# The edges' totals: TensorE makes them one mixing step later, VectorE reads them behind a block of statistics

## The chip, the cores and the metric

One core of one Trainium2 chip runs the whole program. The metric is the device time of one execution in microseconds (us). The kernel before takes 763.93 us (median of three executions, 762.85 to 764.43).

## The reference

The inputs are x (6250 rows of 256 numbers), a graph of 100,000 edges given as `src`, `dst` and `edge_weight`, and weights. Three parts are added up.

```
xn = layernorm(x)
m  = product of 100,000 plane rotations, edge by edge; edges outside the first 256 rows or columns fall away
x1 = x + xn @ m.T + mix(xn)        # mix: K = xn Wk + bk, softmax over the 6250 rows, lambda = softmax(K).T @ (xn Wv + bv),
                                   #      normalised, then (xn Wq + bq) @ lambda
x2 = x1 + moe(layernorm(x1))       # 8 experts, the top 2 of each row, 256 -> 512 -> 256
```

Only edges with an end below 256 change the rotation matrix. So the kernel first sorts out which of the 100,000 edges count, numbers them, and gathers their records; that is the "edge work" of the first part. The change lies there.

## The kernel before

Each engine has its own list of instructions, written out by hand, and the lists meet at semaphores. Nothing reorders them: an instruction that waits holds back all that stands behind it on its engine.

**The mixing steps.** The rows of x are taken in 13 groups, group 0 of 106 rows and groups 1 to 12 of 512. For a group q:

- VectorE makes the mean and variance of the rows (`row_stats`, line 1302 for the statistics, line 1305 to combine them; `xld2` and `xld3` are the third and fourth blocks of eight row tiles of x).
- ScalarE turns the variance into a scale (`deviations`), and normalises the rows (`norm_rows`, line 981).
- TensorE transposes the normalised rows (`turn_in`, line 2199), and multiplies them with the key weights (`keys`, line 2208).
- VectorE takes the running maximum of the keys (`maxima`, lines 1337 to 1347; line 1346 writes `ebias`, for which ScalarE waits), ScalarE takes the exponentials (`exps`, line 1029), TensorE transposes them (`turn_exps`, line 2219), ScalarE moves them to SBUF (`turned_exps`, line 1019), and TensorE multiplies them with the rows (`weigh`, line 2229).
- VectorE adds that product to a running sum (`weighted_sum`, line 1360), which frees the PSUM bank.

TensorE's `mix_step(q)` is `turn_exps(q)`, `keys(q+1)`, `turn_in(q+2)`, then a piece of edge work in some steps, then `weigh(q)`. `weigh(q)` waits until `weighted_sum(q-1)` of VectorE has emptied the bank. VectorE's `mix_step(q)` is `weighted_sum(q-1)`, `sum_exps(q)` (lines 1351 to 1354), `maxima(q+1)`. Edge work stands between the mixing steps on VectorE as well.

**The edge work around the change.** VectorE counts, in each of up to 125 partitions, the edges that matter (`count_rest`, `count_head`, the last instruction being the scan of line 1399). TensorE makes the totals over the partitions with eight small matmuls against a triangle and against ones (`totals`, line 2237), into the first four columns of the bank `misc`. VectorE copies the four columns to SBUF and compares two of them with bounds (`take_counts`: line 1404, then lines 1406 and 1407). GpSimd waits for that copy (`TOTALLED`). It adds the totals to the numbers of the edges (lines 747 and 748), reports `ENDS`, and goes on with passes over all 100,000 edges (lines 750, 751, 726, 727, 726, 727, 731, 757). VectorE's `split_ends` (lines 1412 to 1416) waits for `ENDS`; `hist_columns(0)` (line 1420, 125 x 3200) follows it, and `mix_step(2)` follows that.

In the order of TensorE before, `totals` stands in step 1:

```
for q = 1:  turn_exps(1)  keys(2)  turn_in(3)  totals()  weigh(1)
for q = 2:  turn_exps(2)  keys(3)  turn_in(4)  weigh(2)
```

Later, in step 5, TensorE makes `pair_totals` (line 2261) by six matmuls of one column each, which are like those of `totals`. ScalarE takes sines and cosines of all edges ahead of `end_step(4)`; GpSimd gathers records once VectorE's `number_blocks` is done in step 4.

Of the kernel before, what the change touches and what calls it, by code (L numbers as in the profile page):

```python
# [21 lines left out]
def gnn_layer(nc, x, src, dst, edge_weight, W_qk, b_qk, W_v, b_v, bn_gamma, bn_beta,  # L22
              gamma, beta, Wr, br, W1, b1, W2, b2, out):

    N, D = x.shape
    NE = src.shape[0]
    NX, _, H = W1.shape
    KB = D // P
    NT = (N + P - 1) // P
# [52 lines left out]
    with ctx:  # L82
# [300 lines left out]
        S = {}  # L383
# [905 lines left out]
        def _(dve):  # L1289
# [8 lines left out]
            def row_stats(loaded, lo, hi):  # L1298

                dve.wait_ge(S[loaded], 16)  # L1300
                for t in range(lo, hi):
                    last = nc.vector.bn_stats(stats[:, t, :], x_all[:, t, :])  # L1302
                own(last)
                for t in range(lo, hi):
                    last = nc.vector.bn_aggr(mv[:, t, :], stats[:, t, :])
                return last
# [25 lines left out]
            def maxima(q):  # L1332
                W = width(q)
                n0 = q * PERM + base
                dve.wait_ge(S["keys_psum"], q + 1)
                for kb in range(KB):
                    last = nc.vector.reduce_max(grp_m[:, kb:kb + 1], bank[2 + kb][:, 0:W], AX_X)
                last.then_inc(S["dve"], 1)
                dve.wait_ge(S["dve"], n0 + 1)
                at_least(dve, S["exp_done"], q)  # L1340
                STT(new_m[:, :], run_m[:, :], 1.0, grp_m[:, :], ALU.mult, ALU.max).then_inc(S["dve"], 1)
                dve.wait_ge(S["dve"], n0 + 2)
                STT(dm[:, :], run_m[:, :], 1.0, new_m[:, :], ALU.mult, ALU.subtract)
                STT(ebias[:, :], bk_c[:, :], 1.0, new_m[:, :], ALU.mult, ALU.subtract).then_inc(S["dve"], 1)
                dve.wait_ge(S["dve"], n0 + 3)
                STT(ebias[:, :], ebias[:, :], 1.0, bk_c[:, :], ALU.mult, ALU.subtract).then_inc(S["ebias_ready"], 1)
                STT(run_m[:, :], new_m[:, :], 1.0, new_m[:, :], ALU.mult, ALU.max)

            def sum_exps(q):
                dve.wait_ge(S["exp_done"], q + 1)  # L1350
                STT(ssum[:, :], ssum[:, :], 1.0, alpha[:, :], ALU.mult, ALU.mult).then_inc(S["dve"], 1)
                dve.wait_ge(S["dve"], q * PERM + (base + 4))
                STT(ssum[:, :], ssum[:, :], 1.0, gsum[:, :], ALU.mult, ALU.add)
                STT(alpha2[:, :], alpha[:, :], 1.0, alpha[:, :], ALU.mult, ALU.max).then_inc(S["dve"], 1)
                dve.wait_ge(S["dve"], q * PERM + (base + 5))

            def weighted_sum(q):
                dve.wait_ge(S["mix_psum"], q + 1)
                for kb in range(KB):
                    last = STT(Pacc[:, kb, :], Pacc[:, kb, :], alpha2[:, kb:kb + 1], bank[6][:, kb * D:(kb + 1) * D],  # L1360
                               ALU.mult, ALU.add)
                last.then_inc(S["mix_acc"], 1)
            def mix_step(q):

                if q > 0:
                    weighted_sum(q - 1)
                if q == 4:
                    number_blocks()
                sum_exps(q)
                if q + 1 <= NG12:  # L1370
                    maxima(q + 1)
# [29 lines left out]
            def take_counts():  # L1401

                dve.wait_ge(S["pe"], 1)
                nc.vector.tensor_copy(sums4[:, :], misc[:, 0:4]).then_inc(S["edge_dve"], 1)
                dve.wait_ge(S["edge_dve"], TOTALLED)
                TS(bad[:, 1:2], sums4[:, 2:3], RC * P + 0.5, None, ALU.is_gt)
                TS(bad[:, 2:3], sums4[:, 3:4], HC * P + 0.5, None, ALU.is_gt)

            def split_ends():

                dve.wait_ge(S["edge_pool"], ENDS)
                el(TS(ends_hi[:, :], ends_f[:, :], -(P - 0.5) / 2, 1.0 / P, ALU.add, ALU.mult))
                el(TS(ends_hi[:, :], ends_hi[:, :], MAGIC, None, ALU.add))
                el(TS(ends_hi[:, :], ends_hi[:, :], -MAGIC, None, ALU.add))
                nc.vector.tensor_copy(ends_hi16[:, :], ends_hi[:, :])
                STT(ends_lo[:, :], ends_hi[:, :], -float(P), ends_f[:, :], ALU.mult, ALU.add).then_inc(S["edge_dve"], 1)
                dve.wait_ge(S["edge_dve"], SPLIT)
# [15 lines left out]
            def number_blocks():  # L1433

                dve.wait_ge(S["edge_pe"], BASES)
                el(nc.vector.tensor_copy(counted[:, :], misc[:, 3 * P:3 * P + NCH]))
                for c0, c1 in ((0, HC), (HC, NCH)):
                    last = nc.vector.tensor_tensor_scan(upsum[:, c0:c1], ones[:, 0:1].broadcast_to([P, c1 - c0]), counted[:, c0:c1], 0.0, ALU.mult, ALU.add)
                el(last)
                el(TT(upsum[:, :], upsum[:, :], counted[:, :], ALU.subtract))  # L1440
                TT(block_of[:, :], upsum[:, :], misc[:, 2 * P:2 * P + NCH], ALU.add).then_inc(S["edge_dve"], 1)
# [156 lines left out]
            count_head()  # L1598
            row_stats("xld2", 16, 24)
            mix_step(1)  # L1600
            take_counts()
            row_stats("xld3", 24, 32).then_inc(S["xstats_ok"], 1)
            split_ends()
            hist_columns(0)
            mix_step(2)
# [581 lines left out]
        def _(pe):  # L2187
# [4 lines left out]
            def turn_in(q, b):  # L2192

                W = width(q)
                nt, r = (W + P - 1) // P, W % P or P
                pe.wait_ge(S["xn_ready"], q + 1)
                for kb in range(KB):
                    for t in range(nt):
                        last = tr(bank[kb][:, t * P:t * P + r], xng[b][0:r, t, kb * P:(kb + 1) * P], ident[0:r, 0:r])
                last.then_inc(S["xT_psum"], 1)  # L2200

            def keys(q):
                W = width(q)
                pe.wait_ge(S["xT_done"], q + 1)
                at_least(pe, S["exp_done"], q)
                for db in range(KB):
                    for kb in range(KB):
                        last = mm(bank[2 + db][:, 0:W], wk[:, kb, db * P:(db + 1) * P],  # L2208
                                  xnT[:, kb, bass.ds(tile_at(q) * P, W)], start=(kb == 0), stop=(kb == KB - 1))
                last.then_inc(S["keys_psum"], 1)  # L2210

            def turn_exps(q):

                W = width(q)
                nt, r = (W + P - 1) // P, W % P or P
                pe.wait_ge(S["exp_done"], q + 1)
                for kb in range(KB):
                    for t in range(nt):
                        last = tr(bank[4 + kb][0:r, t * P:(t + 1) * P], ex[:, kb, t * P:t * P + r], ident[:, :])  # L2219
                last.then_inc(S["exT_psum"], 1)  # L2220
# [12 lines left out]
            def totals():  # L2233

                pe.wait_ge(S["edge_dve"], HEAD_SUMMED)
                for c, (left, right, n) in enumerate(((tri, incl, EP), (tri, h_incl, HP), (ones, incl, EP), (ones, h_incl, HP))):
                    last = mm(misc[:, c:c + 1], left[0:n, :], right[:, right.shape[1] - 1:right.shape[1]], start=True, stop=True)
                last.then_inc(S["pe"], 1)

            def histogram():  # L2240

                pe.wait_ge(S["edge_dve"], HIGH)
                for c in range(PH):
                    mm(misc[:, P:P + HC], head_lo[:, c, :], head_hi[:, c, :], start=(c == 0), stop=(c == PH - 1))
                for c in range(PB):
                    last = mm(misc[:, P + HC:P + NCH], hist_lo[c // half_c][:, c % half_c, :], hist_hi[c // half_c][:, c % half_c, :],
                              start=(c == 0), stop=(c == PB - 1))
                last.then_inc(S["edge_pe"], 1)
# [38 lines left out]
            def mix_step(q, b):  # L2287
                turn_exps(q)
                if q + 1 <= NG12:
                    keys(q + 1)  # L2290
                if q + 2 <= NG12:
                    turn_in(q + 2, (b + 2) % 3)
                if q == 1:
                    totals()
                if q == 3:
                    histogram()
                if q == 5:
                    pair_totals()
                weigh(q, b)
# [357 lines left out]
```

## Time and profile before

| what | before |
|---|---|
| median of three executions | 763.93 us |
| the profiled execution | 764.22 us |
| its span, from the first to the last instruction | 762.4 us |
| TensorE busy | 649.5 us (85%) |
| VectorE busy | 508.6 us (67%) |
| ScalarE busy | 443.9 us (58%) |
| GpSimd busy | 407.6 us (53%) |
| mean granted clock of TensorE | 0.921 |

The shares are means over a long kernel. The change touches only some 10 us of it, between 37 and 62 us of the span, so the order of time there says more than the shares do. The chain of waits follows the work that ended last back from the last instruction. The timeline lists one engine's instructions in order of time, and says in brackets how long the engine sat idle ahead of one and what ended that idle time.

### The profile page before, as it was taken

What the parts mean: (1) busy time and instruction counts of PE and PEld (TensorE: products, weight loads), DVE (VectorE), ACT (ScalarE), POOL (GpSimd) and SP (SyncE); (2) the same over time, 40 slices, a digit from 0 to 9 for tenths busy, and PEclk for the clock granted to TensorE, in tenths of its full rate; (3) what the DMA queues carried; (4) which work ended last, traced back from release to release, by engine and by line L of the source; (5) the groups of instructions that cost most, each with busy time, mean ns of one, the idle gap of its engine ahead of it and who ended that gap; (6) DMA issues with size and microseconds to landing.
All of it is one profiled execution on the core that took longest, in us unless ns stands there. A gap on an engine that the chain in (4) does not pass through costs nothing.

```text
span 762.4 us, 18086 instructions
## 1 busy us (share of the span) xinstructions
PE 649.5 (85%) x4055; PEld 552.4 (72%) x4056; DVE 508.6 (67%) x1934; ACT 443.9 (58%) x1218; POOL 407.6 (53%) x494
## 2 busy tenths in 40 slices
PE   6679799944369898807999999999979999999997
PEld 5356467632257666506998999899969999999996
DVE  4999758869957688853454444444446777777775
ACT  6446676557313177844666666566645666666663
POOL 7763777235411237770666677523335666666655
PEclk7879899975579999957999999999999999999999
DMA  6802011415620045562344333322213333333322
GB/s 197 257 2 85 19 33 27 122 52 190 202 71 1 29 144 183 192 209 65 120 141 135 115 131 118 103 69 69 67 63 101 99 104 102 98 103 101 110 91 65
DMA packets 60749, 79.72 MB, mean 105 GB/s; under 512 B 15719, under 2 KB 49381, under 8 KB 60319
## 3 DMA queue, kind: packets, MB, share of 16 engines
q1 hardware_dynamic: 45145, 43.27, 19.6%
q0 software_dynamic: 14976, 35.38, 13.9%
q10 hardware_dynamic: 576, 0.54, 0.2%
q14 instruction: 40, 0.33, 0.1%
q8 instruction: 12, 0.20, 0.1%
HBM read 47.53 MB, written 33.13 MB: 106 GB/s over the span
## 4 chain that ended last, share of the span: by engine, by line
PE 60%; DVE 21%; issue 7%; DMA 4%; ACT 3%; POOL 2%; SPq 1%; DVEq 1%; POOLq 0%; ACTq 0%
PE banks L2601 22%; PE banks L2611 20%; PE banks L2229 4%; PE banks L2208 3%; PE banks L2592 3%; PE banks L2553 2%; DVE R L1997 2%; DVE R L1742 1%; DVE R L1420 1%; DMA R<-in_x_dram 1%; DVE topi L2023 1%; DVE R L1757 1%; DVE R L1302 1%; DMA R<-send_d 1%; PE banks L2219 1%
## 5 line engine op out<-in xcount | busy, mean ns | idle before, releaser
L2601 PE MATMUL banks<-R 128*128 128x128 f32 x1696 | 210.1, 278 | 2.8 <-ACT R L1251 2.8
L2601 PEld LDWEIGHTS banks<-R 128*128 128x128 f32 x1696 | 200.7, 194 | 3.7 <-ACT R L1251 3.6
L2611 PE MATMUL banks<-R 128*128 x848 | 200.7, 380 | 0.0
L1264 ACT ACTIVATE R<-banks,b1c 128x128 f32<-128x128 f32 x424 | 143.5, 365 | 52.0 <-PE banks L2601 51.8
L2611 PEld LDWEIGHTS banks<-R 128*128 128x128 f32 x848 | 153.4, 191 | 16.5
L1251 ACT ACTIVATE R<-banks,bet_c,gam_c 128x128 f32<-128x128 f32 x212 | 85.7, 454 | 106.1 <-PE banks L2592 103.3
L2116 DVE COPY R<-R 128x1024 f32 x106 | 74.5, 702 | 77.2 <-PE banks L2601 60.9
L899 POOL DMA_INDIRECT send_d<-R,slot_all x98 | 97.1, 991 | 48.1 <-issue 40.8
L912 POOL DMA_INDIRECT first_d<-R,dest_now x54 | 60.7, 1123 | 93.3 <-DVE R L2121 81.7
L921 POOL DMA_INDIRECT R<-first_d,get_now x52 | 53.8, 1034 | 50.6 <-DVE get_now L2098 46.3
L912 POOL DMA_INDIRECT out_dram<-R,dest_now x52 | 64.4, 1239 | 30.4 <-issue 27.1
L2229 PE MATMUL banks<-R 128*128 128x256 f32 (+1 forms) x196 | 51.7, 423 | 14.8 <-ACT R L1019 7.4
L2229 PEld LDWEIGHTS banks<-R 128*128 128x128 f32 (+1 forms) x196 | 40.9, 214 | 22.7 <-ACT R L1019 10.3
L2121 DVE TENSOR_TENSOR R<-banks,R 128x256 f32<-128x256 f32 x54 | 22.9, 425 | 49.9 <-PE banks L2611 49.9
L2592 PE MATMUL banks<-ident,R 128*128 128x128 f32 x212 | 41.3, 277 | 15.5 <-DMA R<-send_d 15.5
L2553 PE MATMUL banks<-comb,R 128*128 128x274 f32 (+1 forms) x196 | 51.7, 393 | 0.0
L2592 PEld LDWEIGHTS banks<-ident,R 128*128 128x128 f32 x212 | 29.7, 142 | 27.6 <-DMA R<-send_d 12.2
L2208 PE MATMUL banks<-R 128*128 128x512 f32 (+1 forms) x104 | 46.8, 594 | 0.6 <-ACT R L1009 0.6
L1263 ACT ACTIVATE R<-R 128x256 f32 x106 | 43.3, 408 | 2.7 <-DVE R L2141 2.7
L2110 DVE TENSOR_SCALAR R<-R 128x256 f32<-128x256 f32 x106 | 43.2, 408 | 0.0
L2553 PEld LDWEIGHTS banks<-comb,R 128*128 128x128 f32 (+1 forms) x196 | 33.6, 189 | 9.0
L801 POOL DMA_INDIRECT R<-erec_d,R x33 | 33.8, 1024 | 11.0 <-issue 9.4
(545 smaller groups left out, 998.4 us busy)
## 6 DMA issues: line engine op xcount, KB each, us to landing
R<-send_d SPq DMA_DIRECT2D x106, 131.0 KB
R<-in_L_ffn_W_dram SPq DMA_DIRECT2D x16, 512.0 KB, 4.5
R<-in_x_dram SPq DMA_DIRECT2D x14, 512.0 KB, 4.3
R<-in_x_dram SPq DMA_DIRECT2D x5, 1024.0 KB, 10.8
send_d<-zrow SPq DMA_DIRECT2D x14, 131.0 KB, 2.4
send_d<-R,slot_all POOLq DMA_INDIRECT x98, 3.1
erec_d<-R SPq DMA_DIRECT2D x1, 1400.0 KB
rec_d<-R SPq DMA_DIRECT2D x1, 1400.0 KB
```

The lines of the kernel that those rows point to most:

```text
L899: nc.gpsimd.indirect_dma_start(out=send_d, out_offset=bass.IndirectOffsetOnAxis(ap=slot_all[0:r, t, c:c + 1], axis=0), in_=row_all[0:r, t, ...
L912: nc.gpsimd.indirect_dma_start(out=into, out_offset=bass.IndirectOffsetOnAxis(ap=dest_now[b][:, :], axis=0), in_=yb[b], in_offset=None, bo ...
L921: nc.gpsimd.indirect_dma_start(out=firsts[b], out_offset=None, in_=first_d, in_offset=bass.IndirectOffsetOnAxis(ap=get_now[b][:, :], axis= ...
L1251: last = nc.scalar.activation(xmT[b][:, kb * P:(kb + 1) * P], bank[b][:, kb * P:(kb + 1) * P], ACT.Identity, bias=bet_c[:, kb:kb + 1], sca ...
L1264: last = nc.scalar.activation(hT[b][:, c, :], bank[2 + 2 * b + c // 2][:, (c % 2) * P:(c % 2 + 1) * P], ACT.Gelu, bias=b1c[:, bass.ds(e, 1 ...
L2116: nc.vector.tensor_copy(w1c[b].rearrange("p k h -> p (k h)"), w1s[:, bass.ds(e, 1), :, :].rearrange("p a k h -> p (a k h)"))\
L2208: last = mm(bank[2 + db][:, 0:W], wk[:, kb, db * P:(db + 1) * P], xnT[:, kb, bass.ds(tile_at(q) * P, W)], start=(kb == 0), stop=(kb == KB ...
L2229: last = mm(bank[6][:, kb * D:(kb + 1) * D], exT[0:r, t, kb * P:(kb + 1) * P], xng[b][0:r, t, :], start=(t == 0), stop=(t == nt - 1))
L2553: last = mm(into, xnT[:, kb, at:at + r], comb[:, kb, :], start=False, stop=(kb == KB - 1))
L2592: last = tr(bank[b][:, kb * P:(kb + 1) * P], xm[b][:, kb * P:(kb + 1) * P], ident[:, :])
L2601: last = mm(bank[2 + 2 * b + c // 2][:, (c % 2) * P:(c % 2 + 1) * P], w1c[b][:, kb, c * P:(c + 1) * P], xmT[b][:, kb * P:(kb + 1) * P], st ...
L2611: last = mm(bank[6 + b][:, 0:D], hT[b][:, c, :], w2s[:, bass.ds(e, 1), c, :].rearrange("p a h -> p (a h)"), start=(c == 0), stop=(c == H / ...
```

## The change

`totals()` on TensorE moves from mixing step 1 to step 2. On VectorE `take_counts()` moves behind the statistics of the fourth block of x. No instruction is added or removed; the eight matmuls, the copy and the two comparisons, their waits and their signals are the same.

```
@@ VectorE's list
             row_stats("xld2", 16, 24)
             mix_step(1)
+            row_stats("xld3", 24, 32).then_inc(S["xstats_ok"], 1)
             take_counts()
-            row_stats("xld3", 24, 32).then_inc(S["xstats_ok"], 1)
             split_ends()
             hist_columns(0)
             mix_step(2)
@@ TensorE's mix_step(q, b)
                 if q + 2 <= NG12:
                     turn_in(q + 2, (b + 2) % 3)
-                if q == 1:
+                if q == 2:
                     totals()
                 if q == 3:
                     histogram()
```

## Rows read from the trace of the kernel before

**Rows 1.** Chain of waits, 50 to 84 us: start, duration, engine, tile, line.

```profile
50.35 4.08 DVE R L1420
54.43 0.78 DVE R L1360 x2
70.04 1.34 ACT R L1029 x4
82.37 1.08 ACT R L1019 x2
83.49 6.72 PE banks L2229 x16
```

**Rows 2.** Timeline of TensorE: start, duration, engine, line, operation, out<-in, count, idle before.

```profile
30.83 1.04 PE L2199 MATMUL banks<-ident,R 128*128 128x128 f32 x8
37.30 1.01 PE L2237 MATMUL banks<-R,tri 125*128 125x1 f32 x4 [5.42 <-DVE R L1399]
38.17 0.99 PE L2237 MATMUL banks<-R,ones 125*128 125x1 f32 x4
41.42 5.57 PE L2229 MATMUL banks<-R 128*128 128x256 f32 x16 [2.26 <-DVE R L1360]
...
51.14 1.04 PE L2199 MATMUL banks<-ident,R 128*128 128x128 f32 x8
55.35 5.38 PE L2229 MATMUL banks<-R 128*128 128x256 f32 x16 [3.18 <-DVE R L1360]
```

**Rows 3.** Timeline of TensorE, `pair_totals` and what follows it.

```profile
95.24 0.28 PE L2261 MATMUL banks<-R,tri 125*128 125x1 f32 x2
...
95.83 3.70 PE L2229 MATMUL banks<-R 128*128 128x256 f32 x16
```

**Rows 4.** Timeline of VectorE, 40 to 61 us.

```profile
40.43 0.84 DVE L1360 SCALAR_TENSOR_TENSOR R<-R,alpha,banks 128x256 f32<-128x256 f32 x2
...
43.58 0.15 DVE L1404 COPY sums<-banks 128x4 f32<-128x4 f32 x1
...
43.90 2.70 DVE L1302 BATCH_NORM_STATS2 R<-R 128x6 f32<-128x256 f32 x8
...
47.20 0.16 DVE L1412 TENSOR_SCALAR R<-R 125x55 f32<-125x55 f32 x1
...
48.44 1.75 DVE L1415 CAST R<-R 125x55 bf16<-125x55 f32 x1
...
50.35 4.08 DVE L1420 TENSOR_TENSOR R<-R 125x3200 bf16<-125x3200 bf16 x1
54.35 0.86 DVE L1360 SCALAR_TENSOR_TENSOR R<-R,alpha,banks 128x256 f32<-128x256 f32 x2
55.13 1.04 DVE L1351 SCALAR_TENSOR_TENSOR ssum<-ssum,alpha 128x2 f32<-128x2 f32 x1
...
56.28 1.42 DVE L1354 SCALAR_TENSOR_TENSOR alpha<-alpha 128x2 f32<-128x2 f32 x1
...
59.06 0.63 DVE L1341 SCALAR_TENSOR_TENSOR new_m<-run_m,grp_m 128x2 f32<-128x2 f32 x1
...
59.99 0.16 DVE L1346 SCALAR_TENSOR_TENSOR ebias<-ebias,bk_c 128x2 f32<-128x2 f32 x1
```

**Rows 5.** Timeline of GpSimd, from the totals to its last pass.

```profile
44.37 0.27 POOL L748 TENSOR_SCALAR R<-R,sums 70x5 f32<-70x5 f32 x1
44.84 1.73 POOL L750 TENSOR_SCALAR R<-R,sums 125x800 f32<-125x800 f32 x1 [0.20 <-POOL R L748]
...
58.05 1.63 POOL L757 TENSOR_TENSOR R<-R 125x800 f32<-125x800 f32 x1 [0.18 <-POOL R L731]
```

**Rows 6.** Windows: stretch; busy PE, PEld, DVE, ACT, POOL; PEclk; DMA share; GB/s.

```profile
45.00:46.00 1.00, 1.00 (x6) 0.90 (x5) 1.00 (x4) 0.17 (x2) 1.00 (x1) 0.88 0.00 0
...
54.35:69.90 15.55, 13.50 (x102) 10.13 (x103) 15.17 (x34) 5.62 (x14) 5.05 (x3) 0.89 0.32 104
...
83.40:87.00 3.60, 3.51 (x8) 2.86 (x9) 3.53 (x3) 2.45 (x8) 3.10 (x2) 0.50 0.08 18
```

More of the change, by code:

```diff
@@ L1600, in _ @@
             mix_step(1)
+            row_stats("xld3", 24, 32).then_inc(S["xstats_ok"], 1)
             take_counts()
-            row_stats("xld3", 24, 32).then_inc(S["xstats_ok"], 1)
             split_ends()
@@ L2292, in mix_step @@
                     turn_in(q + 2, (b + 2) % 3)
-                if q == 1:
+                if q == 2:
                     totals()
```

## The prediction

> **What bounds the kernel now.** I read the chain of waits first, because a change of order can only matter where the end of the kernel is set. From 50 us on it runs through VectorE: `hist_columns(0)` at 50.35, the weighted sum at 54.43, then by ScalarE's exponentials at 70.04 to the moved exponentials at 82.37 and TensorE's `weigh(4)` at 83.49 [rows 1]. So in the stretch of the change VectorE sets the end, not TensorE. The windows say the same: of the 15.55 us from 54.35 on VectorE is busy for 15.17 [rows 6]. It has no idle time there in which a delay could vanish.
>
> The timeline of TensorE shows the reverse. It is done with `turn_in(3)` at 31.9, sits 5.42 us until the totals can start, ends them at 39.2, and then sits another 2.26 us until VectorE's weighted sum; `weigh(1)` starts at 41.42. After `turn_in(4)`, which ends at 52.2, it is idle again for 3.18 us, for VectorE's next weighted sum [rows 2]. TensorE is ahead of VectorE, waiting.
>
> The timeline of VectorE gives the order that the change edits: the copy of the totals at 43.58, some 4.4 us after TensorE finished them, with no wait; the statistics of the fourth block from 43.90; `split_ends` from 47.20 [rows 4].
>
> **The change on TensorE, step 1.** Taking the totals out of step 1 removes a wait of 5.42 us and 1.9 us of matmuls. What is late next is the weighted sum: `weigh(1)` must have the bank that VectorE empties in line 1360, and that runs at 40.43 for 0.84 us [rows 4], behind the statistics of the third block. So `weigh(1)` still starts at 41.4, and the removed wait is worth nothing. Its cover is VectorE's order, which the change leaves as it is up to that point.
>
> One side effect can cost. The engine now idles from 31.9 to 41.4 at a stretch. In the trace `weigh(1)` takes 5.57 us and `weigh(2)`, after an idle stretch of 3.18 us, takes 5.38 [rows 2]; `weigh(4)` starts with a granted clock of 0.50 for its first 3.6 us, the 1.2 GHz level, and takes 6.72 us [rows 1, 6]; in `weigh(1)` the clock has risen to a mean of 0.88 by 45 to 46 us [rows 6]. So `weigh(1)` will take between 5.38 and 6.72 us, a cost of -0.2 to +1.15 us. I take +0.5, the mean of the two ends (6.05) less 5.57.
>
> **The change on TensorE, step 2.** Behind `weigh(1)` TensorE has `turn_exps(2)`, `keys(3)` and `turn_in(4)`, all of which have their inputs (`turn_in(4)` ran without a wait), and then the totals. The next matmul after `turn_in(4)` could start at 52.0: rows that follow one another overlap by some 0.15 us, so that is 52.18 less that. Six matmuls of `pair_totals`, of the same kind, take from 95.24 to 95.83 at the high clock, 0.10 us each [rows 3]; eight take 0.8 us. The result is there at 52.9 to 53.0, and VectorE's copy can start at 53.05. With the slower `weigh(1)` that is 53.55. The totals stay ahead of `weigh(2)`, whose input from VectorE comes far later, so their 0.8 us delays nothing on TensorE itself.
>
> **The change on VectorE.** `mix_step(1)` ends at 43.6 as before. The statistics of the fourth block then run 0.3 us earlier and end at 46.9 (3.3 us, from 43.90 to 47.20 [rows 4]). Their signal wakes ScalarE's `deviations(4)`, which by its own order stands behind the end of `weigh(1)`, so earlier is worth nothing. Then the copy of the totals waits for TensorE, from 46.9 to 53.05: 6.1 us of idle time on the engine that sets the end. Queued behind it on VectorE are the two comparisons, `split_ends`, `hist_columns(0)` and the whole of `mix_step(2)`. For the last of these TensorE's `weigh(2)` and ScalarE's `exps(3)` wait. GpSimd waits for the same copy, so its edge passes start as much later as the copy does.
>
> There is a second new wait. `split_ends` needs `ENDS` of GpSimd, which comes when line 748 ends: 44.64, or 1.06 us after the copy starts [rows 4, 5]. Before, the statistics covered it. Now it lies open. `split_ends` and `hist_columns(0)` together took from 47.20 to 54.35, 7.15 us. So the weighted sum starts at 53.05 + 1.06 + 7.15 = 61.26 instead of 54.35, which is **6.9 us later**.
>
> **GpSimd's passes beside VectorE.** Some of VectorE's small instructions were stretched while GpSimd had a pass over the edges. Of `mix_step(2)`, line 1351 took 1.04 us, line 1354 1.42 and line 1341 0.63, where line 1346, on the same 128x2, took 0.16 [rows 4]: 0.9 + 1.25 + 0.45 = 2.6 us lost. The last pass ended at 59.68 [rows 5]. Relative to `ENDS` the passes last 15.0 us, and VectorE spent the first 2.56 of these (44.64 to 47.20) in the statistics, which were not stretched. That cover goes. The bounds are -2.6 us, if no pass meets `mix_step(2)`, and +2.6 us, if all that the statistics covered falls on stretched instructions. Laid side by side with the durations of the trace, `split_ends` and `hist_columns(0)` meet lines 750, 751 and 726 and come out as long as before; `mix_step(2)` then meets lines 727, 726, 727 and 731 in place of 727, 731 and 757, and `ebias` comes 6.8 to 8.0 us after the weighted sum starts, in place of 5.8. I take **+1.2 us**, near the lower end of these 1.0 to 2.2.
>
> The rule behind such stretches in the Trainium skill (SBUF — State Buffer, section on who interferes with whom) is that VectorE and GpSimd share a pair of ports as an exclusive lock: an instruction with two SBUF inputs, or in a two-port mode, is blocked for the whole of a GpSimd instruction that came first, and the statistics, with one input, are not. The cast of line 1415, 1.75 us on 125x55, agrees with it [rows 4]. By the rule the extra is what the alignment gives; without it the extra would be 0, and the forecast 1.2 us lower.
>
> **What comes later.** From the weighted sum on, all chains hang on VectorE: maxima, exponentials, the later edge work, the start of GpSimd's gathers, and by way of ScalarE's sines `weigh(4)`. ScalarE's waits for GpSimd's passes (at 71.4 before) keep their margin: the last pass will end near 69.2, and ScalarE comes there near 80. I find nothing with a start of its own in time that could take the delay up: x is loaded by then, and the gathers start from VectorE's numbers. So the delay is carried whole to the end.
>
> The sum: 0.5 (clock) + 6.9 (the wait, and `ENDS` uncovered) + 1.2 (GpSimd's passes) = +8.6 us. Against the profiled execution of 764.22 that is 772.8. Its span of 762.4 leaves 1.8 us outside, which I leave as it is. The profiled execution is 0.3 us above the median, so for the median I say 772.5.
>
> **The rivals.**
>
> *Part of the delay is taken up later (7 in 100).* TensorE sits idle ahead of `weigh(4)`, and further on in the mixing steps VectorE waits for TensorE. If one of these stretches were tied to something that doesn't move, up to some 5 us would come back. Against it: ahead of `weigh(4)` the chain runs over ScalarE, whose work starts from `exps(4)` and thus from VectorE [rows 1]. The time would be 764.2 + 3.5, so 767.5 or so, in 765.5 to 769.5.
>
> *TensorE gets ahead by the wait that is removed (5 in 100): no slower, or faster.* If `weigh(1)` could start when `turn_in(3)` ends, at 31.9, the totals would stand 10.6 us later (52.0 less 41.42), at 42.5 plus 0.8. They would be ready before the statistics end at 46.9, and VectorE would wait for nothing. Only the uncovered `ENDS` (1.06 us) would stay, and against it up to 2.6 us of stretched instructions could go: 761.5 to 765. It decides from the point at which `weigh(1)` starts by 35.4, for 35.4 + 10.6 + 0.9 is 46.9. For it speaks that TensorE idled longest at the totals. Against it, the row of `weigh(1)` names VectorE's line 1360 as what ended the last wait [rows 2], and that line stands behind the third block's statistics. The start would have to be 6 us earlier than that.
>
> *It costs more (5 in 100).* A `weigh(1)` and a `weigh(2)` at the low clock throughout, and 2.6 us from GpSimd's passes: 0.5 + 1.15 + 6.9 + 2.6 = 11.2, or 775.4, and up to 777.
>
> **How the numbers follow.** The forecast has 83 in 100, with a range of its own of 769.5 to 775 (6.9 alone less some tenths, to 6.9 + 1.15 + 2.6). The range for 8 in 10 is the same, 769.5 to 775, since the rivals hold 17 in 100 among them. A measurement of this kernel tells about 0.2% (1.5 us) from no change. Slower by more: 0.93, from the forecast, the dearer case and nearly all of the first rival with part of the chance of the time in between. Within it: 0.04. Faster by more: 0.03.
>
> **What would show each step.** In the timeline after: `weigh(1)` still starts at 41.4 and ends at 47 to 48; no idle wait for line 1399 at TensorE; totals at 52 to 53.5; VectorE idle some 6 us ahead of line 1404, released by TensorE's line 2237, and 0.8 us ahead of line 1412, released by GpSimd; the weighted sum of `mix_step(2)` at 61 to 62; `weigh(4)` at 92 where it was at 83.49. The prediction is wrong if `weigh(1)` starts clearly before 41, if VectorE waits for the totals by under 3 us, or if `weigh(4)` moves by much less than the weighted sum does.

## The result, and the profile after

The changed kernel takes 769.64 us (median of 19, 763.89 to 773.52), the kernel before, on the same chips, 762.73 us (median of 19, 757.41 to 765.84). The ratio is 1.0106, with a 95% interval of 1.0085 to 1.0128: 8.1 us slower, 6.5 to 9.8. (8.1 us is the centre of this interval; the two medians lie 6.9 us apart.) The forecast was +8.6. Some executions fall in a slower state of the chip; all ratios below, and the time of e10, go by the others alone.

The two profiled executions differ by 2.1 us only (764.22 and 766.33). One reason is that the after one got through the loads earlier: its weighted sum of mixing step 1 starts at 35.91 where it started at 40.43 before [rows 4]. VectorE's statistics of the second block waited for x for 3.54 us before and for 0.56 after, and in the other profiles this weighted sum starts anywhere from 34.92 to 41.66. So I compare stretches counted from this weighted sum, not times from the start.

The chain of waits of the changed kernel, 35 to 89 us (start, duration, engine, tile, line; short stretches of "issue" are left out):

```profile
35.99 0.77 DVE R L1360 x2
36.90 6.58 PE banks L2229 x16
43.48 0.87 PE banks L2219 x8
44.35 3.44 PE banks L2208 x8
47.79 0.87 PE banks L2199 x8
48.66 0.80 PE banks L2237 x8
49.48 0.17 DVE sums L1404
49.83 0.35 POOL R L747
50.28 0.28 POOL R L748
...
53.09 3.49 DVE R L1420
...
60.70 1.49 DVE new_m L1341
...
64.17 1.52 DVE nmr L1319
...
88.58 6.35 PE banks L2229 x16
```

This is the change in one view. Before, the chain ran through VectorE here. Now it crosses to TensorE at `weigh(1)`, goes through all of TensorE's queue ahead of the totals (lines 2229, 2219, 2208, 2199), over the totals and their copy, and on over GpSimd's two small additions to `split_ends` of VectorE, on which it stays until ScalarE's exponentials.

The timeline of TensorE, where `weigh(1)`, the totals, `weigh(2)` and `weigh(4)` answer to [rows 2] and [rows 1]:

```profile
36.90 6.58 PE L2229 MATMUL banks<-R 128*128 128x256 f32 x16 [7.51 <-DVE R L1360]
...
48.50 0.50 PE L2237 MATMUL banks<-R,tri 125*128 125x1 f32 x4
48.86 0.58 PE L2237 MATMUL banks<-R,ones 125*128 125x1 f32 x4
57.51 6.51 PE L2229 MATMUL banks<-R 128*128 128x256 f32 x16 [8.07 <-DVE R L1360]
```

The wait of 5.42 us for line 1399 is gone, and nothing came of it: the idle time ahead of `weigh(1)` is one stretch of 7.51 us, ended as before by VectorE's line 1360. The timeline of VectorE, against [rows 4]:

```profile
41.79 0.64 DVE L1305 BATCH_NORM_AGGREGATE mv<-R 128x2 f32<-128x6 f32 x8
49.48 0.16 DVE L1404 COPY sums<-banks 128x4 f32<-128x4 f32 x1 [7.05 <-PE banks L2237]
...
50.63 0.19 DVE L1412 TENSOR_SCALAR R<-R 125x55 f32<-125x55 f32 x1 [0.73 <-POOLq L749]
...
52.73 0.29 DVE L1415 CAST R<-R 125x55 bf16<-125x55 f32 x1
...
53.09 3.49 DVE L1420 TENSOR_TENSOR R<-R 125x3200 bf16<-125x3200 bf16 x1
56.50 0.87 DVE L1360 SCALAR_TENSOR_TENSOR R<-R,alpha,banks 128x256 f32<-128x256 f32 x2
...
57.47 1.80 DVE L1353 SCALAR_TENSOR_TENSOR ssum<-ssum,gsum 128x2 f32<-128x2 f32 x1
...
62.29 1.42 DVE L1344 SCALAR_TENSOR_TENSOR ebias<-bk_c,new_m 128x2 f32<-128x2 f32 x1
...
64.17 1.52 DVE L1319 SCALAR_TENSOR_TENSOR nmr<-mv,rstd 128x16 f32<-128x16 f32 x1
```

Two waits that were not there, 7.05 us for the totals and 0.73 us for `ENDS`. The instructions around them lie differently against GpSimd's passes: the cast and `hist_columns(0)` are short now, four small instructions of 128x2 and 128x16 long. The timeline of GpSimd, for comparison:

```profile
53.17 4.13 POOL L726 TENSOR_SCALAR R<-R 125x800 f32<-125x800 f32 x1 [0.20 <-POOL R L751]
57.38 1.87 POOL L727 TENSOR_TENSOR R<-R 125x800 f32<-125x800 f32 x1
...
60.29 1.87 POOL L727 TENSOR_TENSOR R<-R 125x800 f32<-125x800 f32 x1
62.25 1.62 POOL L731 TENSOR_SCALAR R<-R 125x800 f32<-125x800 f32 x1
64.05 1.61 POOL L757 TENSOR_TENSOR R<-R 125x800 f32<-125x800 f32 x1 [0.18 <-POOL R L731]
```

Line 1353 of VectorE starts 0.09 us behind the pass at 57.38 and ends with it (57.47 + 1.80 = 59.27, the pass 59.25). Lines 1341 (60.70 to 62.18) and 1319 (64.17 to 65.69) end in the same way with the passes at 60.29 and 64.05 (62.16 and 65.66), and line 1344 ends 0.16 us ahead of the one at 62.25. The weighted sum of step 3, in the changed kernel:

```profile
71.72 0.86 DVE L1360 SCALAR_TENSOR_TENSOR R<-R,alpha,banks 128x256 f32<-128x256 f32 x2
```

and in the kernel before:

```profile
66.62 0.86 DVE L1360 SCALAR_TENSOR_TENSOR R<-R,alpha,banks 128x256 f32<-128x256 f32 x2
```

From the weighted sum of step 1 to that of step 3 it is 35.81 us (71.72 less 35.91), in place of 26.19 (66.62 less 40.43 [rows 4]).

### The profile page after: what moved, and what is told of

The parts are those of the page before. It is cut to its first block, busy times and chain, and to the rows that moved or that the text cites. A ratio compares the mean times of both kernels' runs of the same rounds, so it can differ in the third digit from the quotient of the medians.

```text
span 764.5 us, 18086 instructions
## 1 busy us (share of the span) xinstructions
PE 646.1 (85%) x4055; PEld 549.2 (72%) x4056; DVE 507.8 (66%) x1934; ACT 442.9 (58%) x1218; POOL 406.7 (53%) x494
## 4 chain that ended last, share of the span: by engine, by line
PE 61%; DVE 20%; issue 8%; DMA 4%; ACT 3%; POOL 2%; SPq 1%; DVEq 1%; POOLq 0%; ACTq 0%
PE banks L2601 21%; PE banks L2611 20%; PE banks L2229 5%; PE banks L2208 4%; PE banks L2592 3%; PE banks L2553 2%; DVE R L1997 2%; DVE R L1742 1%; DMA out_dram<-R,dest_now 1%; DVE topi L2023 1%; PE banks L2219 1%; DVE R L1420 1%; DVE R L1757 1%; DMA R<-send_d 1%; DMA R<-in_x_dram 1%
## 5 line engine op out<-in xcount | busy, mean ns | idle before, releaser
L2229 PE MATMUL banks<-R 128*128 128x256 f32 (+1 forms) x196 | 53.4, 433 | 24.4 <-DVE R L1360 17.5
L2592 PEld LDWEIGHTS banks<-ident,R 128*128 128x128 f32 x212 | 29.6, 143 | 27.5 <-DMA R<-send_d 12.6
```

The lines of the kernel that those rows point to most:

```text
L2229: last = mm(bank[6][:, kb * D:(kb + 1) * D], exT[0:r, t, kb * P:(kb + 1) * P], xng[b][0:r, t, :], start=(t == 0), stop=(t == nt - 1))
L2592: last = tr(bank[b][:, kb * P:(kb + 1) * P], xm[b][:, kb * P:(kb + 1) * P], ident[:, :])
```

## The experiments

Times are medians; the ratio is to the kernel before on the same chip. It is the centre of its interval and not the quotient of the two medians: for e11 the medians lie 3.5 us apart and the ratio says 1.0. "Way" is the stretch from the weighted sum of step 1 to that of step 3 in the profile: 26.19 us before, 35.81 changed. The first four ran on a chip where the kernel before took 763.0 us, the next four on one where it took 822.6, the last four on one with 763.65. The 823 us chip is slower later in the program for all kernels, and only ratios and ways are taken from it.

| run | time | ratio (95%) | in us | way | wait ahead of line 1404 |
|---|---|---|---|---|---|
| e1, TensorE's half | 771.15 | 1.0111 (1.0065 to 1.0156) | +8.5 | 36.32 | 10.14 |
| e2, VectorE's half | 765.47 | 1.0035 (1.0003 to 1.0067) | +2.7 | 28.68 | none |
| e3, totals first | 765.76 | 1.0042 (1.0012 to 1.0072) | +3.2 | 30.79 | 2.02 |
| e4, ten more matmuls | 771.89 | 1.0128 (1.0087 to 1.0168) | +9.8 | 37.99 | 9.24 |
| e5, no idle | 830.56 | 1.0093 (1.0056 to 1.0130) | +7.7 | 34.63 | 5.84 |
| e6, warm `weigh(4)` | 821.0 | 0.9992 (0.9967 to 1.0017) | -0.7 | 26.15 | none |
| e7, changed, fewer passes | 826.94 | 1.0051 (1.0020 to 1.0082) | +4.2 | 30.75 | 6.91 |
| e8, before, fewer passes | 818.61 | 0.9952 (0.9918 to 0.9985) | -3.9 | 23.56 | none |
| e9, before, early passes | 764.64 | 1.0009 (0.9978 to 1.0040) | +0.7 | 23.56 | none |
| e10, changed, early passes | 767.2 | 1.0083 (1.0035 to 1.0131) | +6.3 | 30.97 | 4.48 |
| e11, early and warm | 760.15 | 0.9987 (0.9954 to 1.0019) | -1.0 | 26.27 | none |
| e12, e6 again | 761.73 | 0.9974 (0.9951 to 0.9998) | -2.0 | 26.15 | none |

**e1: TensorE's half alone.**

```
-                if q == 1:
+                if q == 2:
                     totals()
```

> TensorE's half of the change alone: totals in mixing step 2, take_counts of VectorE in its old place. Theory W (VectorE's wait for the totals is the cost): the copy of the totals waits from 43.6 to about 53, 9.4 us instead of 6 to 7, and the statistics behind it cover ENDS again, so +9 to +10 us on the kernel before. Rival P (the cost is VectorE's own reordering: ENDS uncovered, GpSimd's passes beside mix_step(2)): without that reordering less than the whole change, +3 us or less. Rival C (the cost is TensorE's clock after the long idle stretch): about the same as the whole change, +7 to +8.

VectorE waits longer than in the whole change, 10.14 us, as the statistics no longer stand ahead of the wait. No wait for `ENDS` is left, and `hist_columns(0)` and line 1351 are as long as before to 0.01 us:

```profile
50.13 0.16 DVE L1404 COPY sums<-banks 128x4 f32<-128x4 f32 x1 [10.14 <-PE banks L2237]
...
53.75 0.16 DVE L1412 TENSOR_SCALAR R<-R 125x55 f32<-125x55 f32 x1
...
56.83 4.08 DVE L1420 TENSOR_TENSOR R<-R 125x3200 bf16<-125x3200 bf16 x1
```

The way grows by 10.13 us, which is the wait of 10.14. Theory P is out. The time alone (+8.5, 5.0 to 11.9) would not have told W from C; the wait does.

**e2: VectorE's half alone.** The same edit the other way round: `take_counts()` moved, `totals()` in step 1.

> VectorE's half alone: take_counts behind the statistics of the fourth block, totals of TensorE in step 1 as before. Theory W: no wait for the totals; only ENDS lies open (+0.8 net) and GpSimd's passes meet mix_step(2) (+1.2), so +2.0 us, 0.8 to 3.5, on the kernel before. Rival P: +5 us or more. Rival C: 0.

```profile
46.39 0.12 DVE L1404 COPY sums<-banks 128x4 f32<-128x4 f32 x1
...
47.50 0.19 DVE L1412 TENSOR_SCALAR R<-R 125x55 f32<-125x55 f32 x1 [0.74 <-POOLq L749]
```

The way grows by 2.5 us, the time by 2.7 (0.2 to 5.1). So of the 9.6 us of the whole change 2.5 come from VectorE's order and 7.1 from the wait of 7.05. The two halves run alone add up to more, 12.6 us, since in e1 the statistics no longer hide 3.1 us of the wait. The 2.5 us are 0.45 us less up to step 2, although 0.74 us of waiting for `ENDS` is in there, and 2.9 us more from step 2 to step 3.

**e3: the totals first in step 2.**

```
             def mix_step(q, b):
+                if q == 2:
+                    totals()
                 turn_exps(q)
...
-                if q == 2:
-                    totals()
                 if q == 3:
```

> The whole change, but totals at the head of TensorE's mixing step 2, ahead of turn_exps(2), keys(3) and turn_in(4), which take 5.2 us. Theory W: the wait ahead of line 1404 falls by 4.5 to 5 us, to about 2.3, and the time is 4.7 us below the changed kernel, +3.4 us on the kernel before. Rival P and rival C: as the changed kernel, +7 to +8, since VectorE's order and TensorE's idle stretch ahead of weigh(1) are the same.

```profile
41.54 6.73 PE L2229 MATMUL banks<-R 128*128 128x256 f32 x16 [7.29 <-DVE R L1360]
48.10 0.50 PE L2237 MATMUL banks<-R,tri 125*128 125x1 f32 x4
```

TensorE's idle stretch and its slow `weigh(1)` are those of the changed kernel, but the wait is 2.02 us and the way 30.79: 5.03 us of wait less, 5.02 us of way less. This also bounds theory C: with the same clock most of the cost is gone.

**e4: the other way.** Ten idle matmuls of `ident` ahead of the totals.

> The whole change with ten idle 128x128 matmuls of ident ahead of the totals, whose product nobody reads (20 records of 0.115 us at the high clock, 2.3 us). Theory W: VectorE's wait grows by 2.3 us and the kernel by the same, +10.4 us on the kernel before. Rival (part of the delay is taken up later): less than 1.2 us above the changed kernel. Rival C: no more than the changed kernel, as TensorE's idle stretch ahead of weigh(2) only gets shorter.

The wait is 9.24 us, 2.19 more than in the changed kernel, and the way 2.18 longer. Four wait lengths (0, 2.02, 7.05, 9.24) with VectorE's new order give ways of 28.68, 30.79, 35.81 and 37.99: the way is 28.7 plus the wait, to 0.1 us. In the time the step from the changed kernel is +1.7 us, 2.3 were expected; the interval of e4 (6.6 to 12.8) is too wide to confirm it or to exclude the rival.

**e5: TensorE kept busy.** In step 1 28 idle matmuls after `turn_in(3)`, in step 2 26 more after the copy of the totals.

> The whole change with idle matmuls of ident that fill TensorE's two idle stretches: 28 in step 1 after turn_in(3), 26 in step 2 once VectorE has copied the totals. Their product is read by nobody. Theory C (part of the cost is the low clock after idle time): weigh(1) takes 3.7 us in place of 6.58, the totals come 2.9 us earlier, VectorE's wait falls from 7.05 to about 4.2, and the kernel gains 2.9 us on the changed one (+5.2 us on the kernel before). Rival: the clock there costs nothing, because some other wait holds the totals; then the time is that of the changed kernel, +8.

```profile
31.70 6.42 PE L2295 MATMUL banks<-ident 128*128 128x128 f32 x56
40.93 5.38 PE L2229 MATMUL banks<-R 128*128 128x256 f32 x16 [2.81 <-DVE R L1360]
```

The experiment half missed: the filling ended 2.81 us before `weigh(1)` could start, and the granted clock, 1.00 until 41 us, fell again (the windows show 0.60 from 41 to 43 us). `weigh(1)` took 5.38 us in place of 6.58, the wait 5.84 in place of 7.05, and the way 34.63 in place of 35.81: again one for one. So what `weigh(1)` takes less at the higher clock, 1.2 us here, is gained through the wait. The time (+7.7, 4.6 to 10.7) can't show that; it agrees with the theory and with the rival.

**e7 and e8: four of GpSimd's passes left out.** The angles miss the second and third parts of the whole turns.

```
             whole_turns(turn, theta)
             less_part(turn, theta, part_turn, TURN_HI)
...
-            less_part(turn, theta, part_turn, TURN_MID)
-            less_part(turn, theta, part_turn, TURN_LO)
```

> The changed kernel without four of GpSimd's passes over all edges: the second and third parts of the whole turns are not taken off the angles (lines 726 and 727, twice), so the angles are slightly off. Theory: GpSimd's passes stretch VectorE's small instructions of mix_step(2); without four of them mix_step(2) gets shorter by 2.5 to 3.5 us here. Against the same kernel with the old order (the next one) it is +6.5 to +7.5 us, which is the pure wait. Rival: the passes cost nothing, the time is that of the changed kernel (+8 on the kernel before) and the difference to the next one is 8.

> The kernel before without the same four passes of GpSimd. In its trace the stretched instructions of mix_step(2) lose 2.6 us and hist_columns(0) some 0.6 more; theory: -2 to -3 us on the kernel before. Rival: the stretched instructions are not on the path, 0.

In the old order the way falls by 2.63 us, in the new one by 5.06. Without the passes the change costs 7.19 us of way, with them 9.62: their share in it is 2.4 us. That the passes cost time shows in the times as well, -3.9 us for e8 (-6.7 to -1.2). The difference between e7 and e8 in the times is 8 us, with an interval too wide to tell 7.2 from 9.6.

**e9 and e10: the same passes, early.** The four passes go ahead of GpSimd's wait for the totals, where it sat idle for 8.5 us. Nothing is left out.

```
+            less_part(turn, theta, part_turn, TURN_MID)
+            less_part(turn, theta, part_turn, TURN_LO)
             pool.wait_ge(S["edge_dve"], TOTALLED)
```

> The kernel before with four of GpSimd's passes (lines 726 and 727, twice) moved ahead of its wait for the totals, into 8.5 us in which it sat idle; nothing is left out. Theory (the passes cost by stretching VectorE's instructions of mix_step(2), which sets the end): the way from the weighted sum of step 1 to that of step 3 falls from 26.2 to 23.6 us, and the kernel gains 2.5 to 3.7 us on the kernel before. Rival: the passes now stretch mix_step(1) as much, 0.

> The changed kernel with the same four passes moved ahead of GpSimd's wait for the totals. Theory: the change costs 7.2 us by VectorE's waits and 2.4 us more by the passes; with the passes out of the way the way between the two weighted sums falls from 35.8 to 30.8 us and the kernel is 3 to 4.5 us slower than before. Rival (the passes cost nothing extra in the changed order): +5 us or more.

The way is what was expected for both (23.56 and 30.97). The time of e9 is not: +0.7 (-1.7 to +3.1), where a gain of 2.5 to 3.7 us was expected. That of e10, +6.3 (2.7 to 10.0), holds the theory's 3 to 4.5 and the rival's 5 alike. In the profile of e9 the passes stand beside `count_head`, ahead of the way:

```profile
33.62 1.86 DVE L1397 SCALAR_TENSOR_TENSOR R<-R 70x79 f32<-70x79 f32 x1
35.52 0.90 DVE L1398 SCALAR_TENSOR_TENSOR R<-R 70x80 f32<-70x80 f32 x1
36.45 2.01 DVE L1399 TENSOR_TENSOR_SCAN R<-ones,R 70x80 f32<-70x80 f32 x1
```

These three took 0.23, 0.24 and 0.32 us in the kernel before: 4 us more here. Other instructions of `count_head` were long in the kernel before, line 1391 with 1.93 us for one, so the two profiles don't balance to the tenth; that the gain was given back there is the likely reading, not a shown one. Behind that point this profile keeps the gain: from the weighted sum of step 1 to the last instruction it is 3.0 us shorter than the kernel before.

Where the loads come early the passes fall beside `mix_step(1)` instead. That is so in the profile of e10, where a line 1351 took 1.69 us; its `mix_step(1)` is 2.6 us longer, and the wait for the totals, down to 4.48 from 7.05, hides nearly all of it. It is so in the profile of e11 below as well, which has VectorE's old order and no such wait: its way is 26.27 us, against 23.56 in e9 and 26.19 before. There the whole gain is gone, as e9's rival had it.

**e6, e12 and e11: a `weigh(4)` at the high clock.** This came out of [rows 1] and [rows 6]: `weigh(4)` is on the chain and took 6.72 us.

```
+                if q == 4:
+                    pe.wait_ge(S["edge_dve"], BLOCKS)
+                    for _ in range(22):
+                        mm(misc[:, 3 * P:4 * P], ident[:, :], ident[:, :], start=True, stop=True)
                 weigh(q, b)
```

> The kernel before with 22 idle matmuls of ident in TensorE's step 4, after number_blocks and ahead of weigh(4), in the 5.6 us for which TensorE waits for ScalarE; nobody reads their product. If the low clock of weigh(4) (6.72 us, on the chain) is a cost of its own, weigh(4) takes 3.7 us and the kernel becomes 2.5 to 3 us faster than before. Rival: weigh(4)'s length is covered by VectorE's edge work, which ends at 89.4 where weigh(4) ends at 90.2: then under 1 us.

> The kernel before with the four early passes and the 22 idle matmuls ahead of weigh(4). If both gains are there and add up: 4.5 to 6 us faster than the kernel before. Rival: weigh(4)'s gain is taken up by a later wait, then as the early passes alone, -2.5 to -3.7.

> The kernel before with the 22 idle matmuls ahead of weigh(4) once more, beside the others. In the first trace of it weigh(4) took 3.72 us in place of 6.72 and weigh(5) started 2.3 us earlier, but the time did not show it. Theory: -2.3 us. Rival: the gain is lost behind weigh(5): within 1 us of the kernel before.

The timeline of TensorE in e12:

```profile
77.18 5.08 PE L2298 MATMUL banks<-ident 128*128 128x128 f32 x44
82.95 3.72 PE L2229 MATMUL banks<-R 128*128 128x256 f32 x16 [0.69 <-ACT R L1019]
...
92.28 3.70 PE L2229 MATMUL banks<-R 128*128 128x256 f32 x16
```

`weigh(4)` takes 3.72 us and `weigh(5)` starts 52.4 us after the weighted sum of step 1, in place of 55.4 (95.83 less 40.43). e12 is 2.0 us faster than the kernel before (0.2 to 3.7), the only version with nothing left out whose interval excludes no gain, and only just; e6, the same program, says -0.7 (-2.7 to +1.4), which agrees with e12 and also with no gain. Part of the 3.0 us is lost behind `weigh(5)`: in the profile of e12, counted from the weighted sum of step 1, the last weighted sum of the mixing steps comes 0.75 us earlier than before and the end 1.4 us earlier.

e11 says -1.0 (-3.5 to +1.5), where 4.5 to 6 us were expected: the two gains don't add up. In its profile the way is as long as before, and `weigh(4)`, straight behind the idle matmuls, starts 44.98 us after the weighted sum of step 1, later than the 43.06 before.

## Why the prediction was right

**The wait moved, and nothing was gained by its removal: right.** `weigh(1)` started 0.99 us after the weighted sum began, as before (41.42 less 40.43).

**The clock: +0.5 forecast, +1.0 in this pair of traces** (6.58 less 5.57 us), between the bounds, near the upper one. The granted clock is 0.50, the 1.2 GHz level, from 36.9 to 40 us, and e5 shows that what `weigh(1)` takes more or less reaches the way through the wait one for one. That the longer idle stretch is what made it slower is shown less well. With TensorE's old order `weigh(1)` took 5.54 to 6.73 us over seven traces (before, e2, e6, e8, e9, e11, e12; mean 6.09), with the totals moved 6.36 to 6.73 over six (after, e1, e3, e4, e7, e10; mean 6.51). By the means the term is 0.4 us, within the scatter of the old order; the pair alone makes it 1.0.

**The wait and `ENDS`: right in kind.** Forecast were waits of 6.6 us (with the clock) and 0.8; measured 7.05 and 0.73. What I had wrong there was `split_ends` with `hist_columns(0)`: 5.87 us (50.63 to 56.50), not the 7.15 of before, which I had laid side by side as unchanged. Together, the weighted sum of step 2 came 6.67 us later, counted from that of step 1, where 7.4 was forecast.

**GpSimd's passes: +1.2 forecast, too low for what comes after that sum.** For `ebias` the reckoning held: it comes 7.4 us after the weighted sum starts (56.50 to 63.90), in place of 5.8, within the forecast 6.8 to 8.0. But from step 2 to step 3 the changed kernel needs 15.22 us in place of 12.27, 2.95 more. Lines 1353, 1341, 1344 and 1319 took 1.80, 1.48, 1.42 and 1.52 us. On `hist_columns(0)` it was GpSimd that waited: it started 0.08 us ahead of GpSimd's line 726, which took 4.13 us from 53.17 on. Line 1415 took 0.29 us in place of 1.75 and line 1420 3.49 in place of 4.08, line 1413 1.62 in place of 0.79: the 1.3 us above. Net it is 1.7 us against 1.2. My side-by-side reckoning left out line 1319, which follows `mix_step(2)` and alone makes 1.3 us.

The rule cited from the Trainium skill held in kind: the statistics, with one input, were 2.68 to 2.71 us in every order, and small instructions with two inputs ended with the pass that had started first. Lines 1413 and 1415 have one input each and were long too (1.62 us beside GpSimd's line 750, 1.75 beside line 727 before); by the rule these would be the two-port mode, which no run here shows. e7 against e8 gives the share of the four passes in what the change costs, 2.4 us of way.

**Carried whole to the end: nearly.** `weigh(4)` starts 52.67 us after the weighted sum of step 1, in place of 43.06: 9.6 later. The last weighted sum of the mixing steps (163.79, before 159.05) is 9.3 later, and the measured time 8.1, with an interval of 6.5 to 9.8 that holds both. `weigh(4)` itself gave 0.4 of this back (6.35 us in place of 6.72). Counted from the same weighted sum to the last instruction, this pair of profiles differs by 6.6 us only; where the other 2.7 went I don't know. The profiles of e1 to e4 keep their delay: +9.3, +2.9, +3.5 and +12.0 us at the last weighted sum, +9.0, +3.5, +2.9 and +12.6 at the last instruction. So nothing behind the mixing steps takes it up as a rule.

The sum was +8.6 by +0.5, +6.9 and +1.2; by the trace it is +9.6 on the way, 6.7 up to step 2 (7.4 forecast) and 2.95 behind it (1.2 forecast). So a part of the good fit is that errors cancelled.

**The time itself: inside the range by luck.** For the median I had said 772.5, in 769.5 to 775; 769.64 is 2.9 us below the one and 0.14 us inside the other. The difference of 8.1 us fits much better than that. The median of the kernel before is 762.73 us over 19 executions, where I had started from 763.93 over three.

**The rivals.** That TensorE would get ahead is excluded by the row of `weigh(1)`. That up to 5 us would be taken up later is excluded for the way by its own 9.6 us and by e3 and e4; for the end of the kernel the interval leaves up to 3.1 us of it (9.6 less 6.5). Of the dearer case one half came: `weigh(2)` took 6.51 us in place of 5.38. It cost nothing, as TensorE waited for ScalarE's exponentials for another 1.50 us behind it.

## What to carry to other kernels

Before moving work to "fill a wait", ask who waits last. TensorE's 5.4 us wait for VectorE cost nothing, since the next thing in its queue waited for the same engine anyway; moving the totals behind 11 us of queued work made the engine that sets the end wait for TensorE. A result that one engine makes and another reads is cheap only while its maker's queue stands shorter than its reader's; count the queue ahead of it (here: `weigh(1)`, `turn_exps(2)`, `keys(3)`, `turn_in(4)`).

Statistics behind a copy are a cover for what a third engine does with that copy. And when two traces of a noisy kernel are compared, count from an event that both share.

## What the hardware showed that I had not expected

A filling that stopped 2.81 us before the next matmuls did not keep the clock: `weigh(1)` still took 5.38 us, where the same 16 matmuls take 3.7 at the high level [rows 3]. With a gap of 0.69 us (e12) it was kept. The gap right ahead doesn't decide alone: in the same e12 `weigh(1)` took 6.37 us after 2.26 us of idle time, with 3.56 us more ahead of the totals, and `weigh(2)` took 3.69 us after 2.36.

Moving GpSimd's passes into its own idle time gained nothing (e9, +0.7 us, -1.7 to +3.1), although leaving them out gained 3.9 us: the stretch moved to other instructions of VectorE, from 0.32 to 2.01 us in the case of line 1399. Where a pass falls differs with the loads: in e9 and e11, whose lists are the same up to step 4, GpSimd's early passes start within 0.2 us of each other (33.52 and 33.67 for the first line 727), and VectorE's weighted sum of step 1 at 41.66 and 36.01.

The same programs took 60 us more on one chip (822.6 against 763 us). Up to the weighted sum of step 3 the profiles agree to 0.05 us (e6 and e12: a way of 26.15 us each, 26.19 before). Later, in the mixing steps of e6, TensorE sat idle for 7.72 and 11.78 us ahead of lines 2199 and 2229, with no releaser that the profile shows. What that is stays open.
